# A graph network on one core: the last stage with its gate combined three groups ahead

## The chip, the core and the metric

The kernel runs on one core of a Trainium2 chip. A core has TensorE (matmuls and transposes into PSUM), VectorE, ScalarE and GpSimd (elementwise work), and SyncE, which here issues plain DMAs. GpSimd also issues the indirect DMAs (gathers and scatters by row numbers). Each engine runs its own list of instructions in order and waits on semaphores for the others. The metric is the device time of the whole kernel in microseconds. In the profile PE is TensorE, PEld its weight loads, DVE VectorE, ACT ScalarE, POOL GpSimd, SP SyncE.

## What is computed

Two layers of a heterogeneous graph transformer over 6250 nodes of width 128 and 100000 edges, with 16 node types and 32 edge types, and at the end a dense layer, a sum with the input and a layer norm. What matters here is what is done to each node once the sums over its edges are there:

```python
h = silu(typed_linear(hag, ntype, Wa))        # hag: attention-weighted messages, summed by node
alpha = sigmoid(skip[ntype])[:, None]
h = h * alpha + x * (1.0 - alpha)
mu, var = mean(h), mean((h - mu) ** 2)
h = (h - mu) * rsqrt(var + 1e-05) * g + b
...                                            # after the second layer:
out = layernorm(x_input + h @ ff_w + ff_b)
```

## The kernel before

The nodes are sorted by type and padded to 64 tiles of 128 nodes, so that a tile has one type and a typed linear map is one matmul with a weight picked by the type. A fused pass makes tables and queries of a layer, and an attention pass (`attend`) goes over the edges. After the second layer's attention comes the last stage, the functions named `finish` of each engine. It works on 16 groups of 4 tiles (`GROUP`, `GROUPS`). The change lies in this stage alone.

For a group g the stage does, engine by engine, in the names of the code:

- SyncE `load(g)`: three loads (edge sums, h of the layer before, x) into a ring of 8 places. From group 8 on it waits for the sum with x of group g - 8.
- VectorE `divide_in(g)` (L1666 to L1668): divides the sums by their totals.
- TensorE `turn_in(g)` (L1274): four transposes; ScalarE `turn_in(g)` (L1007) copies them out of PSUM bank 0; TensorE `project_in(g)` (L1282): the typed linear map.
- ScalarE `scale_o_res(g)` (L1022): h of before times 1 - alpha, four instructions; ScalarE `gate(g)` (L1029): the tanh that the silu is made of.
- VectorE `combine(g)` (L1812, L1817, and `statistics` with L1673, L1677, L1679): gate, residual, mean and variance.
- GpSimd `power` (L807): one instruction raises variances to the power -1/2. It takes up to two of them at once: the layer's, of a group ahead, and the output's, of group g.
- VectorE `shift(g)` (L1825): minus mean times that power; ScalarE `centre(g)` (L999): the normalised rows, four instructions.
- TensorE `turn_hn(g)` (L1291): four transposes; ScalarE `turn_hn(g)` (L1013) copies them from bank 2 with g and b; TensorE `spread_bias(g)` (L1297), a matmul with one row that puts the bias into the output's bank, and `project_out(g)` (L1303), the dense layer.
- VectorE `add_x(g)` (L1833 and `statistics`): the sum with x and its mean and variance; the output's half of `power(g)`; VectorE `output_shift(g)` (L1842); ScalarE `normalise(g)` (L1036), four instructions; GpSimd `scatter(g)` (L813), four indirect DMAs.

The order is written out by hand: on each engine a loop over steps i calls these functions for groups at different distances from i. In step i VectorE adds x of group i and combines group i + 2; TensorE and ScalarE turn in group i + 3 and turn out group i + 1; power(i) takes the output's variance of group i and the layer's of group i + 2. `wait_ge(semaphore, n)` holds an engine until n increments are there; `wait(engine, semaphore, n)` does so where n is positive.

Of the kernel before, what the change touches and what calls it, by code (L numbers as in the profile page):

```python
# [24 lines left out]
GROUP = 4  # L25
GROUPS = SORTED_TILES // GROUP
# [35 lines left out]
EPS = 1e-5  # L62
# [28 lines left out]
def gnn_kernel(nc, x, src, dst, etype, ntype, Wk, Wq, Wv, Wa, Watt, Wmsg, pri, skip, ln_g, ln_b, ff_w, ff_b, out):  # L91
# [5 lines left out]
    with ctx:  # L97
# [604 lines left out]
        def _(pool):  # L702
# [92 lines left out]
            def finish():  # L795

                def power(g):

                    layer, output = g + 2 < GROUPS, g >= 0
                    if layer:  # L800
                        pool.wait_ge(var_ready, GROUPS + g + 3)
                        wait(pool, hn_ready, GROUPS + g + 1 if g >= 0 else 0)
# [14 lines left out]
                for i in range(-2, GROUPS + 2):  # L817
                    if 0 <= i - 2 < GROUPS:
                        scatter(i - 2)
                    if i < GROUPS:  # L820
                        power(i)
# [55 lines left out]
        def _(act):  # L877
# [112 lines left out]
            def finish():  # L990
# [3 lines left out]
                def centre(g):  # L994
# [3 lines left out]
                    for t in range(GROUP):  # L998
                        ins = nc.scalar.activation(o_hn[:, g % 2, t], o_h[:, g % 3, t], ACT.Identity,  # L999
                                                   scale=rstd[:, g % 2, 0, t:t + 1], bias=hn_shift[:, g % 2, t:t + 1])  # L1000
# [40 lines left out]
                for i in range(-3, GROUPS + 2):  # L1041
                    if real(i + 1):
                        centre(i + 1)
                    if real(i + 3):
                        turn_in(i + 3)
                    if real(i + 1):
                        turn_hn(i + 1)
                    if real(i + 3):
                        scale_o_res(i + 3)
                        gate(i + 3)  # L1050
                    if real(i - 1):
                        normalise(i - 1)

# [60 lines left out]
        def _(pe):  # L1114
# [149 lines left out]
            def finish():  # L1264
# [42 lines left out]
                for i in range(-3, GROUPS):  # L1307
                    if real(i + 3):
                        types = tile_types((i + 3) * GROUP, GROUP)
                        turn_in(i + 3)  # L1310
                    if real(i + 1):
                        turn_hn(i + 1)
                    if real(i + 3):
                        project_in(i + 3, types)
                    if real(i + 1):
                        spread_bias(i + 1)
                        project_out(i + 1)
# [103 lines left out]
        def _(dve):  # L1421
# [248 lines left out]
            def statistics(par, kind, tiles, mean_var_, ready):  # L1670
# [8 lines left out]
                v.tensor_scalar(var_eps[:, par, kind], mean_var_[:, par, :, 1], EPS, None, ALU.add).then_inc(ready, 1)  # L1679
# [118 lines left out]
            def finish():  # L1798
# [7 lines left out]
                def combine(g):  # L1806
# [12 lines left out]
                    statistics(g % 2, 0, lambda t: hh[:, t], mean_var, var_ready)  # L1819
# [248 lines left out]
```

## Time and profile before

| | |
|---|---|
| median of 3 runs | 3597.92 us (3592.7 to 3605.9) |
| the profiled execution | 3599.04 us, its span 3597.2 us |
| mean granted TensorE clock | 0.843 |
| busy in the span: VectorE, GpSimd, TensorE | 76%, 69%, 69% |
| last stage, first load to end of span | 3429.75 to 3597.2 us |
| issued in it: group 3's and group 15's turn_in copy | 3454.87 and 3550.68 us |

A row of a timeline gives start, duration, engine, line, operation and tiles, how many instructions of a kind in a row are put together, and in square brackets how long the engine was idle before it and what ended that. The granted clock (PEclk) is 1.00 at 2.4 GHz and 0.50 at 1.2 GHz. Busy times of matmuls can overlap a little, as their ends are modelled.

### The profile page before, as it was taken

What the parts mean: (1) busy time and instruction counts of PE and PEld (TensorE: products, weight loads), DVE (VectorE), ACT (ScalarE), POOL (GpSimd) and SP (SyncE); (2) the same over time, 40 slices, a digit from 0 to 9 for tenths busy, and PEclk for the clock granted to TensorE, in tenths of its full rate; (3) what the DMA queues carried; (4) which work ended last, traced back from release to release, by engine and by line L of the source; (5) the groups of instructions that cost most, each with busy time, mean ns of one, the idle gap of its engine ahead of it and who ended that gap; (6) DMA issues with size and microseconds to landing.
All of it is one profiled execution on the core that took longest, in us unless ns stands there. A gap on an engine that the chain in (4) does not pass through costs nothing.

```text
span 3597.2 us, 61645 instructions
## 1 busy us (share of the span) xinstructions
PE 2472.3 (69%) x14287; PEld 1814.4 (50%) x14288; DVE 2746.2 (76%) x6153; ACT 1893.1 (53%) x4824; POOL 2474.7 (69%) x2501
## 2 busy tenths in 40 slices
PE   2777777467767767667677777657777776767665
PEld 1333333356666656666333333346666665666543
DVE  7667677488888878787687888758888888888765
ACT  1667677145444544545576767615445445544555
POOL 3666665677777777774566666477777777777746
PEclk8889988688888888888799999868888888888866
DMA  7999999655555545445799999955554555555350
GB/s 152 404 391 395 373 391 401 214 151 146 150 151 152 147 140 144 137 140 147 196 407 382 383 371 374 400 177 138 143 142 140 143 143 141 143 140 142 92 154 33
DMA packets 331216, 783.28 MB, mean 218 GB/s; under 512 B 87275, under 2 KB 262267, under 8 KB 318335
## 3 DMA queue, kind: packets, MB, share of 16 engines
q0 software_dynamic: 106016, 638.52, 49.5%
q1 hardware_dynamic: 216371, 139.98, 14.8%
q8 instruction: 139, 2.28, 0.3%
q14 instruction: 242, 1.98, 0.2%
q10 hardware_dynamic: 8448, 0.53, 0.2%
HBM read 335.84 MB, written 573.22 MB: 253 GB/s over the span
## 4 chain that ended last, share of the span: by engine, by line
POOL 26%; DMA 20%; issue 20%; DVE 11%; PE 10%; ACT 5%; DVEq 5%; POOLq 3%; ACTq 0%; SPq 0%
POOL region L836 21%; DMA relation_table<-region,scatter_node 13%; DMA region<-relation_table,key_of 5%; PE bank L1178 4%; ACT region L924 3%; DVEq L1893 3%; POOLq L831 2%; PE bank L1345 2%; DVEq L1901 1%; DMA region_q<-sums_by_node,gather_node 1%; DVE region_q L1873 1%; POOL aggregated_rows L848 1%; PE bank L1208 1%; POOL region_q L741 1%; DVE region L1887 1%
## 5 line engine op out<-in xcount | busy, mean ns | idle before, releaser
L836 POOL DMA_INDIRECT region<-relation_table,key_of x1568 | 1567.7, 1000 | 501.0 <-issue 442.2
L1345 PE MATMUL bank<-region,arena 128*128 128x136 f32 x3968 | 717.9, 335 | 255.4 <-ACT arena L1063 146.6
L1345 PEld LDWEIGHTS bank<-region,arena 128*128 128x128 f32 x3968 | 620.9, 231 | 333.9 <-issue 221.6
L924 ACT COPY region<-bank 128x512 f32<-128x512 f32 x1152 | 621.9, 599 | 285.8 <-DMA relation_table<-region,scatter_node 167.2
L1690 DVE COPY region<-bank 128x512 f32<-128x512 f32 x896 | 585.9, 685 | 209.2 <-DMA relation_table<-region,scatter_node 121.1
L1178 PE MATMUL bank<-sums,arena 128*128 128x512 bf16 x2048 | 620.5, 414 | 172.8 <-ACT region L924 142.8
L1060 ACT ACTIVATE arena<-iota_free,minus_dst 128x128 f32<-128x128 f32 x1984 | 629.0, 387 | 168.1 <-PE bank L1345 166.1
L1334 PE MATMUL bank<-region_q 128*128 x3968 | 640.6, 315 | 78.0 <-DVE region_q L1873 54.0
L1334 PEld LDWEIGHTS bank<-region_q 128*128 128x128 f32 x3968 | 604.3, 232 | 85.5 <-issue 85.4
L1864 DVE TENSOR_TENSOR bank<-bank,region 128x512 f32<-128x512 f32 x496 | 346.0, 698 | 363.9 <-POOLq L844 193.2
L1068 ACT ACTIVATE region<-arena 128x32 f32<-128x32 f32 x496 | 106.6, 215 | 949.7 <-DVE arena L1977 938.7
L1178 PEld LDWEIGHTS bank<-sums,arena 128*128 128x128 bf16 x2048 | 194.1, 102 | 498.9 <-ACT region L924 222.6
L1887 DVE TENSOR_TENSOR region<-region 128x512 f32<-128x512 f32 x496 | 338.0, 681 | 19.8 <-issue 11.1
L1878 DVE TENSOR_REDUCE arena<-bank 128x32 f32<-128x512 f32 x496 | 335.7, 677 | 0.0
L1063 ACT ACTIVATE arena<-arena 128x512 f32<-128x512 f32 x496 | 312.4, 630 | 15.7
L1873 DVE TENSOR_SCALAR region_q<-arena,row_no 128x512 f32<-128x512 bf16 x496 | 245.9, 497 | 39.8 <-issue 19.8
L757 POOL TENSOR_TENSOR sums<-arena,sums 128x256 f32<-128x256 f32 x128 | 86.2, 673 | 230.1 <-ACT arena L942 229.6
L1378 PE MATMUL bank<-ident,arena 128*1 128x128 f32 x496 | 124.8, 409 | 104.0 <-DVE arena L1942 104.0
L1697 DVE COPY arena<-bank 128x1024 bf16<-128x1024 bf16 x256 | 175.5, 685 | 22.3 <-PE bank L1199 15.5
L1199 PEld LDWEIGHTS bank<-identb,sums 128*128 128x128 bf16 x2048 | 151.8, 106 | 56.1 <-issue 17.6
L1199 PE MATMUL bank<-identb,sums 128*128 128x128 bf16 x2048 | 174.8, 234 | 2.6 <-POOL sums L761 2.6
L774 POOL DMA_INDIRECT relation_table<-region,scatter_node x128 | 126.2, 986 | 70.2 <-issue 35.1
(299 smaller groups left out, 2801.9 us busy)
## 6 DMA issues: line engine op xcount, KB each, us to landing
arena<-edge_places SPq DMA_DIRECT2D x496, 128.0 KB, 3.2
region<-relation_table,key_of POOLq DMA_INDIRECT x1568, 3.0
arena<-segment_flags SPq DMA_DIRECT2D x124, 128.0 KB
region_q<-q_rows SPq DMA_DIRECT2D x6, 768.0 KB, 15.7
aggregated_rows<-one_less_alpha SPq DMA_DIRECT2D x17, 256.0 KB, 4.0
region<-aggregated_rows SPq DMA_DIRECT2D x16, 272.0 KB, 3.1
sums<-relation_weight_parts SPq DMA_DIRECT2D x32, 128.0 KB, 9.9
x_sorted<-arena SPq DMA_DIRECT2D x16, 256.0 KB, 13.6
```

Source lines behind the costliest of these rows:

```text
L836: pool.indirect_dma_start(out=rows[:, r, s], out_offset=None, in_=table, in_offset=bass.IndirectOffsetOnAxis(ap=key_of[:, n:n + 1], axis=0 ...
L924: nc.scalar.copy(stage[:, r, :, k * HS:(k + 1) * HS], bank[TABLE_BANK + k % TABLE_BANKS][:, :].rearrange("p (t o) -> p t o", t=RT)).then_i ...
L1060: chain.step(nc.scalar.activation(onehots[:, at, s], iota_free[:, :], ACT.Abs, bias=minus_dst[:, bass.ds(block_.b * BLOCK + (q * QUAD + s) ...
L1063: nc.scalar.activation(onehots[:, at], onehots[:, at], ACT.Relu, scale=-1.0, bias=1.0).then_inc(onehot_ready, 1)
L1178: nc.tensor.matmul(bank[TABLE_BANK + k % TABLE_BANKS][:, :], x_spreadT[:, k, :], w_rel[:, k, :], start=True, stop=True).then_inc(table_psu ...
L1199: ins = nc.tensor.transpose(bank[SPREAD_BANK[half]][:, :].bitcast(BF16)[:, k * P:(k + 1) * P], x_spread[:, tile.par, half * H + k].rearran ...
L1334: ins = nc.tensor.matmul(bank[Q_BANK[at]][:, s * D:(s + 1) * D], onehotT[:, at, s], q_rows[:, bass.ds(tile, 1), :].rearrange("p a n -> p ( ...
L1345: ins = nc.tensor.matmul(bank[SUM_BANK[q % SUM_RING]][:, 0:SUMC], onehots[:, at, s], weighed_rows[:, weighed_at, s, :], start=(s == 0), st ...
L1690: v.tensor_copy(stage[:, r, :, k * HS:(k + 1) * HS], bank[TABLE_BANK + k % TABLE_BANKS][:, :].rearrange("p (t o) -> p t o", t=RT)).then_in ...
L1864: v.tensor_tensor(fetched, fetched, rows[:, bass.ds(read, 1), :, 0:D].rearrange("p r s d -> p (r s) d"), ALU.mult).then_inc(prod_ready, 1)
L1878: v.tensor_reduce(score[:, block_.par, q * QUAD:(q + 1) * QUAD, :], bank[Q_BANK[q_place(block_, q)]][:, :].rearrange("p (s h o) -> p s h o ...
L1887: v.tensor_tensor(part[:, :, H:SUMC].rearrange("p s (h o) -> p s h o", h=H), msg, bc(part[:, :, 0:H], 3, HS), ALU.mult).then_inc(weighted, 1)
```

## The change

Three things, all in the last stage. Combine, and with it the layer's half of the power, is done three groups ahead of the output instead of two (and `divide_in` five ahead instead of four, TensorE's and ScalarE's turning in four ahead instead of three, their turning out two ahead instead of one). On VectorE the two shifts stand behind the sum with x instead of in front of it. And the order within a step of TensorE and ScalarE is another. Since a power now holds an output of group g and a layer of group g + 3, the layer's place in `var_eps` and `rstd` has the other parity.

```diff
@@ GpSimd, finish @@
-                    layer, output = g + 2 < GROUPS, g >= 0
+                    layer, output = g + 3 < GROUPS, g >= 0
                     if layer:
-                        pool.wait_ge(var_ready, GROUPS + g + 3)
-                        wait(pool, hn_ready, GROUPS + g + 1 if g >= 0 else 0)
+                        pool.wait_ge(var_ready, GROUPS + g + 4)
+                        wait(pool, hn_ready, GROUPS + g + 2 if g >= -1 else 0)
...
-                for i in range(-2, GROUPS + 2):
+                for i in range(-3, GROUPS + 2):
@@ ScalarE, finish @@
-                                                   scale=rstd[:, g % 2, 0, t:t + 1], bias=hn_shift[:, g % 2, t:t + 1])
+                                                   scale=rstd[:, (g + 1) % 2, 0, t:t + 1], bias=hn_shift[:, g % 2, t:t + 1])
...
-                for i in range(-3, GROUPS + 2):
-                    if real(i + 1):
-                        centre(i + 1)
-                    if real(i + 3):
-                        turn_in(i + 3)
-                    if real(i + 1):
-                        turn_hn(i + 1)
-                    if real(i + 3):
-                        scale_o_res(i + 3)
-                        gate(i + 3)
+                for i in range(-4, GROUPS + 1):
+                    if real(i + 4):
+                        turn_in(i + 4)
+                        scale_o_res(i + 4)
+                    if real(i + 2):
+                        centre(i + 2)
+                    if real(i + 4):
+                        gate(i + 4)
                     if real(i - 1):
                         normalise(i - 1)
+                    if real(i + 2):
+                        turn_hn(i + 2)
@@ TensorE, finish @@
-                for i in range(-3, GROUPS):
-                    if real(i + 3):
-                        types = tile_types((i + 3) * GROUP, GROUP)
-                        turn_in(i + 3)
-                    if real(i + 1):
-                        turn_hn(i + 1)
-                    if real(i + 3):
-                        project_in(i + 3, types)
-                    if real(i + 1):
-                        spread_bias(i + 1)
-                        project_out(i + 1)
+                for i in range(-4, GROUPS):
+                    if real(i + 4):
+                        types = tile_types((i + 4) * GROUP, GROUP)
+                        turn_in(i + 4)
+                        project_in(i + 4, types)
+                    if real(i + 2):
+                        turn_hn(i + 2)
+                        spread_bias(i + 2)
+                        project_out(i + 2)
@@ VectorE, finish @@
-                    dve.wait_ge(rstd_ready, GROUPS + g + 3)
+                    dve.wait_ge(rstd_ready, GROUPS + g + 4)
...
-                for i in range(-4, GROUPS + 1):
-                    if real(i + 1):
-                        shift(i + 1)
-                    if real(i - 1):
-                        output_shift(i - 1)
+                for i in range(-5, GROUPS + 1):
                     if real(i):
                         add_x(i)
                     if real(i + 2):
-                        combine(i + 2)
-                    if real(i + 4):
-                        divide_in(i + 4)
+                        shift(i + 2)
+                    if real(i - 1):
+                        output_shift(i - 1)
+                    if real(i + 3):
+                        combine(i + 3)
+                    if real(i + 5):
+                        divide_in(i + 5)
```

What stands in a row on ScalarE in one step of the middle of the stage, before (L1007 is turn_in, L1013 turn_hn, L1022 scale_o_res, L1029 gate, L1036 normalise, L999 centre; in brackets the semaphores waited for):

```order
L999 ACTIVATE region<-region,rstd 128x128 [waits hnT_psum,hn_shifted]
L999 ACTIVATE region<-region,rstd 128x128 x3
L1007 COPY region<-bank 128x512 [waits z_psum,inT_psum]
L1013 ACTIVATE region<-bank,affine 128x512 [waits out_psum,hnT_psum]
L1022 ACTIVATE region<-region,one_less_alpha 128x128 [waits layer_const_ready,rows_loaded3]
L1022 ACTIVATE region<-region,one_less_alpha 128x128 x3
L1029 ACTIVATE region<-bank 128x512 [waits z_used,z_psum]
L1036 ACTIVATE region<-region,out_shift,rstd 128x128 [waits scattered1,norm_ready]
L1036 ACTIVATE region<-region,out_shift,rstd 128x128 x3
```

And after, on ScalarE, from the end of one step over the next:

```order
L1013 ACTIVATE region<-bank,affine 128x512 [waits out_psum,hnT_psum]
L1007 COPY region<-bank 128x512 [waits z_psum,inT_psum]
L1022 ACTIVATE region<-region,one_less_alpha 128x128 [waits layer_const_ready,rows_loaded4]
L1022 ACTIVATE region<-region,one_less_alpha 128x128 x3
L999 ACTIVATE region<-region,rstd 128x128 [waits hnT_psum,hn_shifted]
L999 ACTIVATE region<-region,rstd 128x128 x3
L1029 ACTIVATE region<-bank 128x512 [waits z_used,z_psum]
L1036 ACTIVATE region<-region,out_shift,rstd 128x128 [waits scattered1,norm_ready]
L1036 ACTIVATE region<-region,out_shift,rstd 128x128 x3
L1013 ACTIVATE region<-bank,affine 128x512 [waits out_psum,hnT_psum]
L1007 COPY region<-bank 128x512 [waits z_psum,inT_psum]
```

The copy of turn_hn (L1013) has moved from the third place to the last of its step, directly in front of the next step's turn_in (L1007).

On TensorE, before, from the spread of one step on (L1274 is turn_in, L1291 turn_hn, L1282 project_in, L1297 spread_bias, L1303 project_out):

```order
L1297 MATMUL bank<-row_const,ones 128x512 [waits y_ready]
L1303 MATMUL bank<-region_q,region 128x128 [waits hnT_ready]
L1303 MATMUL bank<-region_q,region 128x128 x3
L1159 TENSOR_LOAD tile_type
L1274 MATMUL bank<-ident,region 128x128 [waits inT_ready,in_ready]
L1274 MATMUL bank<-ident,region 128x128 x3
L1291 MATMUL bank<-ident,region 128x128 [waits hnT_ready,hn_ready]
L1291 MATMUL bank<-ident,region 128x128 x3
L1282 ISA [waits z_used,inT_ready]
L1282 MATMUL bank<-region_q,region 128x128
```

And after, on TensorE, the same place:

```order
L1291 MATMUL bank<-ident,region 128x128 [waits hnT_ready,hn_ready]
L1291 MATMUL bank<-ident,region 128x128 x3
L1297 MATMUL bank<-row_const,ones 128x512 [waits y_ready]
L1303 MATMUL bank<-region_q,region 128x128 [waits hnT_ready]
L1303 MATMUL bank<-region_q,region 128x128 x3
L1159 TENSOR_LOAD tile_type
L1274 MATMUL bank<-ident,region 128x128 [waits inT_ready,in_ready]
L1274 MATMUL bank<-ident,region 128x128 x3
L1282 ISA [waits z_used,inT_ready]
L1282 MATMUL bank<-region_q,region 128x128
```

The transposes of turn_hn no longer stand between those of turn_in and project_in, but behind project_in.

## Rows read from the trace of the kernel before

**Rows 1.** Windows of the fill and the steady part: window, length, busy, clock, DMA.
```profile
core 0: us, PE busy (x) PEld busy (x) DVE busy (x) ACT busy (x) POOL busy (x), PEclk, DMA share, GB/s
3429.00:3456.00 27.00, 16.07 (x60) 12.54 (x61) 13.13 (x50) 11.64 (x29) 2.05 (x2) 0.50 0.82 241
3456.00:3551.00 95.00, 69.11 (x309) 49.04 (x309) 79.32 (x349) 71.11 (x176) 61.73 (x54) 0.77 0.31 91
```

**Rows 2.** Timeline of VectorE over one period: start, us, instructions, idle before.
```profile
3533.48 0.16 DVE L1825 SCALAR_TENSOR_TENSOR region<-mean_var,rstd 128x4 f32<-128x4 f32 x1 [0.59 <-POOL rstd L807]
...
3539.92 0.69 DVE L1668 TENSOR_TENSOR region<-region 128x512 f32<-128x512 f32 x1
3541.20 0.16 DVE L1825 SCALAR_TENSOR_TENSOR region<-mean_var,rstd 128x4 f32<-128x4 f32 x1 [0.59 <-POOL rstd L807]
```

**Rows 3.** Timeline of ScalarE over one period at the full clock.
```profile
3536.07 0.78 ACT L1013 ACTIVATE region<-bank,affine 128x512 f32<-128x512 f32 x1 [0.28 <-PE bank L1291]
3536.75 1.26 ACT L1022 ACTIVATE region<-region,one_less_alpha 128x128 f32<-128x128 f32 x4
3537.92 0.57 ACT L1029 ACTIVATE region<-bank 128x512 f32<-128x512 f32 x1
3538.40 1.64 ACT L1036 ACTIVATE region<-region,out_shift,rstd 128x128 f32<-128x128 f32 x4
3541.40 1.65 ACT L999 ACTIVATE region<-region,rstd 128x128 f32<-128x128 f32 x4 [1.37 <-DVE region L1825]
3542.95 0.56 ACT L1007 COPY region<-bank 128x512 f32<-128x512 f32 x1
```

**Rows 4.** Timeline of TensorE over one period at the full clock.
```profile
3535.38 0.65 PE L1291 MATMUL bank<-ident,region 128*128 128x128 f32 x4 [1.78 <-ACT region L999]
3535.95 1.15 PE L1282 MATMUL bank<-region_q,region 128*128 x8
...
3540.66 0.66 PE L1274 MATMUL bank<-ident,region 128*128 128x128 f32 x4 [1.43 <-DVE region L1668]
```

**Rows 5.** Timeline of TensorE and ScalarE at the half clock, two places.
```profile
3451.91 2.08 PE L1303 MATMUL bank<-region_q,region 128*128 128x128 f32 x8
...
3453.78 1.06 PE L1274 MATMUL bank<-ident,region 128*128 128x128 f32 x4
...
3454.87 0.59 ACT L1007 COPY region<-bank 128x512 f32<-128x512 f32 x1 [2.60 <-PE bank L1274]
...
3557.20 1.65 ACT L999 ACTIVATE region<-region,rstd 128x128 f32<-128x128 f32 x4 [1.26 <-DVE region L1825]
...
3558.90 1.12 PE L1291 MATMUL bank<-ident,region 128*128 128x128 f32 x4 [1.25 <-ACT region L999]
...
3559.95 2.07 PE L1297 MATMUL bank<-row_const,ones 1*128 1x512 f32 x2
...
3561.94 2.08 PE L1303 MATMUL bank<-region_q,region 128*128 128x128 f32 x8
```

**Rows 6.** Timeline: transposes of group 2, and group 15's turn_in copy.
```profile
3445.34 1.12 PE L1274 MATMUL bank<-ident,region 128*128 128x128 f32 x4 [1.73 <-DVE region L1668]
...
3550.68 0.56 ACT L1007 COPY region<-bank 128x512 f32<-128x512 f32 x1
```

**Rows 7.** Timeline of GpSimd in the tail.
```profile
3563.51 1.67 POOL L807 TENSOR_TENSOR rstd<-var_eps,minus_half 128x8 f32<-128x8 f32 x1 [1.40 <-DVE var_eps L1679]
3565.38 1.04 POOL L813 DMA_INDIRECT out_dram<-region,scatter_node  x1 [0.20 <-issue]
...
3576.45 1.07 POOL L807 TENSOR_TENSOR rstd<-var_eps,minus_half 128x4 f32<-128x4 f32 x1
3577.71 1.04 POOL L813 DMA_INDIRECT out_dram<-region,scatter_node  x1 [0.19 <-issue]
...
3586.72 0.97 POOL L813 DMA_INDIRECT out_dram<-region,scatter_node  x1 [0.30 <-issue]
```

**Rows 8.** Windows of two stretches at the half clock, columns as in rows 1.
```profile
3511.00:3520.00 9.00, 8.59 (x31) 6.45 (x32) 6.94 (x32) 6.98 (x17) 6.68 (x6) 0.50 0.40 121
...
3545.00:3575.00 30.00, 21.92 (x64) 13.74 (x64) 18.72 (x89) 18.40 (x45) 21.88 (x20) 0.50 0.07 26
```

More of the change, by code:

```diff
@@ L1668, in divide, with statistics @@
                 v.tensor_tensor(messages, messages, bc(total, 3, HS), ALU.mult).then_inc(in_ready, 1)
-            def statistics(par, kind, tiles, mean_var_, ready):
+            def statistics(par, kind, at, tiles, mean_var_, ready):
                 for t in range(GROUP):
@@ L1678, in statistics @@
                 chain.wait()
-                v.tensor_scalar(var_eps[:, par, kind], mean_var_[:, par, :, 1], EPS, None, ALU.add).then_inc(ready, 1)
+                v.tensor_scalar(var_eps[:, at, kind], mean_var_[:, par, :, 1], EPS, None, ALU.add).then_inc(ready, 1)
             def fused(l):
@@ L1818, in combine @@
                     chain.wait()
-                    statistics(g % 2, 0, lambda t: hh[:, t], mean_var, var_ready)
+                    statistics(g % 2, 0, (g + 1) % 2, lambda t: hh[:, t], mean_var, var_ready)
                 def shift(g):
@@ L1824, in shift @@
                     wait(dve, hn_ready, GROUPS + g - 1 if g >= 2 else 0)
-                    v.scalar_tensor_tensor(hn_shift[:, g % 2], mean_var[:, g % 2, :, 0], -1.0, rstd[:, g % 2, 0],
+                    v.scalar_tensor_tensor(hn_shift[:, g % 2], mean_var[:, g % 2, :, 0], -1.0, rstd[:, (g + 1) % 2, 0],
                                            ALU.mult, ALU.mult).then_inc(hn_shifted, 1)
@@ L1835, in add_x @@
                     dve.wait_ge(y_ready, g + 1)
-                    statistics(g % 2, 1, lambda t: y[:, t], out_mean_var, out_var_ready)
+                    statistics(g % 2, 1, g % 2, lambda t: y[:, t], out_mean_var, out_var_ready)
                 def output_shift(g):
-                    dve.wait_ge(rstd_ready, GROUPS + g + 3)
+                    dve.wait_ge(rstd_ready, GROUPS + g + 4)
                     wait(dve, out_ready, g - 1)
```

## The prediction

> **What bounds the kernel now.** I read the windows by stage first. The change touches only the last stage, from the loads at 3429.75 us to the end at 3597.2 us; the 3430 us before it run the same instructions. It has a fill at the half clock up to 3456, a steady part of 95 us and a tail. In the steady part VectorE is busy 79.3 us, ScalarE 71.1, TensorE 69.1, GpSimd 61.7 [rows 1], so several engines are nearly full and none is.
>
> Next I read the timeline of VectorE in one period. L1825 starts at 3533.48 after 0.59 us of idle time that ends with GpSimd's power, and again at 3541.20 after 0.59 [rows 2]. The period is 7.72 us, of which VectorE works from 3533.48 to the end of L1668 at 3540.61, that is 7.13. So in this stretch the path goes round VectorE and GpSimd: combine's variance, power (1.67 us, the first row of [rows 7]), shift, sum with x, combine. This is the wait the change removes. The copies of turn_in on ScalarE start at 3454.87 for group 3 [rows 5] and at 3550.68 for group 15 [rows 6]: 95.81 us for 12 periods, 7.98 on average. The excess over 7.72 comes with TensorE's lower clock. The granted clock averages 0.77 in the steady part [rows 1], and as it has only the levels 1.0 and 0.5 there (2.4 and 1.2 GHz), it was full in 0.27/0.50 = 54% of that time: some 6.7 periods of 7.72, so that the other 5.3 took 8.3 each.
>
> **What the change removes.** Combine of group g+3 now stands before power(g), and after combine VectorE has divide_in and the sum with x (over 3 us of the 7.13) before it needs the power. 1.67 us are covered, so the 0.59 us go. What would be late next on VectorE alone is its own work: 7.13 us plus some 0.02 of handover, 7.15 a period. The sum of VectorE's instructions is unchanged, and so is GpSimd's (one power more in the fill, and of the last output powers three instead of two have no layer part).
>
> **What it adds: a ring between ScalarE and TensorE.** ScalarE's row of a period is now turn_in, scale, centre, gate, normalise, turn_hn. TensorE's is turn_in, project_in, turn_hn, spread, project_out. Before, ScalarE's turn_hn copy stood third, with scale, gate and normalise behind it to cover project_out. Now it is the last of the step. TensorE's project_out waits for it; the next turn_in transposes are queued behind project_out; ScalarE's next turn_in copy waits for these transposes, and everything else of ScalarE is queued behind that copy. Nothing on either engine overlaps this stretch, whatever VectorE does, so one turn of the ring is a floor for the period.
>
> One turn at the full clock, start to start, from [rows 3, 4]. The ScalarE instructions overlap the next by 0.09 (gate is 0.57 long, 0.48 to the next): turn_in 0.56 - 0.09 = 0.47; scale 1.17 (3536.75 to 3537.92); centre 1.55 (3541.40 to 3542.95); gate 0.48; normalise, four instructions like centre's, 1.55; turn_hn to its end 0.78. That is 6.00. Handover to TensorE 0.05 (as from centre's end, 3557.20 + 1.65 = 3558.85, to L1291 at 3558.90, [rows 5]). project_out has the eight passes of L1282, busy 1.15, of which some 0.07 overlap the next instruction: 1.08. Transposes until the copy starts: 0.69 (L1291 at 3535.38, L1013 at 3536.07). Sum 6.00 + 0.05 + 1.08 + 0.69 = 7.82 us. This is 0.1 above the 7.72 of before: the wait for GpSimd is gone and a slightly longer one stands in its place.
>
> At the half clock a second way round is longer [rows 5]: turn_in 0.47, scale 1.17, centre until TensorE's transposes start 1.70 (3557.20 to 3558.90), transposes 1.05, spread 1.99 (3559.95 to 3561.94), project_out 1.87 (3451.91 to 3453.78), transposes until the copy 1.09 (3453.78 to 3454.87). Sum 9.34 us. By the first way it would be 6.00 + 0.05 + 1.87 + 1.09 = 9.01, so 9.34 decides; at the full clock the second way, with its four TensorE pieces halved, is the shorter one. Before, a period with this clock in it cost 8.3, because turn_in's and turn_hn's copies were both covered by TensorE's other work.
>
> **What is moved past queues.** On GpSimd a power stands between two groups of scatters as before. SyncE's load of group 8 waits for the sum with x of group 0, and divide_in of group 8 is now three steps behind that sum instead of four: three periods, over 20 us, still cover it. ScalarE's centre waits for VectorE's shift, which now stands behind the sum with x; in the ring VectorE has 7.82 - 7.15 = 0.7 us to spare a period and gets ahead of ScalarE, so I cost it at nothing; if that cover went, VectorE's own 7.15 us a period would bound, which is the third rival.
>
> **How often the clock is full.** That is the unknown of the sum. In the kernel before it rose behind stretches in which TensorE had hardly a gap, such as 3511 to 3520 with 8.59 us busy of 9.00 [rows 8], where turn_in, turn_hn, project_in and project_out of neighbouring steps run into one another. It fell where one short group of transposes stands between two idle times, 1.4 and 1.8 us in every full-clock period [rows 4]. In the tail, with 21.9 us busy of 30, it never rose [rows 8]. After the change, at the half clock, TensorE works 1.05 + 1.9 + 1.05 + 1.99 + 1.87 = 7.9 us of 9.34, and the rest is cut into two gaps, one for turn_in's copy before project_in and one for centre before turn_hn: no stretch of the step is as dense as 3511 to 3520, in any period. At the full clock these pieces halve and three gaps lie between them. I expect it to be mostly at 1.2 GHz. The ends are 12 periods at half (9.34) and the share of before, 1/(0.54/7.82 + 0.46/9.34) = 8.45. I take 9 periods at half and 3 at full, 107.5 us for 12, nearer to the upper end.
>
> The Trainium skill, "TensorE: Matmul & The Clock Gate" (HAM oscillation), says that the clock falls when TensorE has long idle gaps and stays up when work is issued without them. By that alone the change should help, for its gaps are shorter. Here it fell with gaps of 1.4 and 1.8 us and stayed low in a tail that was 73% busy, so the trace does not bear the rule out, and it stands behind the second rival below.
>
> **Fill.** Transposes of group 2 start at 3445.34 [rows 6], as before; the copy can start at 3445.34 + 1.09 = 3446.4 (no centre in front of it now). One turn at half clock brings group 3's copy to 3455.8, against 3454.87 before: 0.9 later.
>
> **Tail.** From group 15's copy on. Before: copy at 3550.68, last scatter issued by 3586.72 + 0.97 = 3587.69, 37.0 us, then 9.5 us to the end of the span, which stays. After: turn_in of group 15 is in step 11 and not 12, so six groups are still to be scattered from there. Normalise of group 10 is done 0.47 + 1.17 + 1.55 + 0.48 + 1.64 = 5.3 us behind the copy. Then GpSimd is the bound [rows 7]: four scatters take 4 x 1.287 = 5.15 (3577.71 to 3586.72 is seven spacings); six groups 30.9; power 12 with two parts 1.87 (3563.51 to 3565.38); powers 13 to 15 with one part 1.26 each (3576.45 to 3577.71), 3.8. Sum 5.3 + 30.9 + 1.9 + 3.8 - 0.3 (the last spacing) = 41.6 us.
>
> **Sum.** 3455.8 + 107.5 + 41.6 + 9.5 = 3614.4 us span, 17.2 over 3597.2. The profiled execution took 3599.04, so 3616.2 by its own time; over the median of 3597.92 it is 3615.1. I forecast 3616, slower by 0.5%. What a measurement of this kernel can tell from no change is about 0.5%, 18 us: the bound is 3615.9 and my forecast sits on it.
>
> **Rivals.** All with the same fill and tail, 3506.9 + 12 periods, and 0.7 added to the median.
> - The clock keeps its share of before: 12 x 8.45 = 101.4, span 3608.3, time 3609. For it: TensorE's work per period is the same. Against: the broken dense stretch.
> - The clock stays full once up, as shorter gaps could bring about: 12 x 7.82 = 93.8, span 3600.7, time 3601.5. For it: the longest gap is shorter. Against: it fell in [rows 1] with gaps of the same size. The rule cited above gives this case.
> - The ring does not bind and the work of VectorE does: 12 x 7.15 = 85.8, span 3592.7, time 3593.5, not slower, 0.1% faster. It needs the next turn_in transposes to be done without waiting for project_out, and decides if one turn is under 7.15. Against: [rows 5] show L1274 starting only behind L1303, and the waits are in the program's order.
> - The ring binds and the clock never rises, with a few tenths a period of jitter on top: 12 x 9.34 = 112.1 gives 3619.0, with 0.4 more each 3623.8; time 3620 to 3625.
>
> **How the numbers follow.** Forecast, 0 to 4 periods at full clock around the 9 at half: 0.60, own range 3611 to 3621, a bit more than half of it above 3615.9. Clock share as before 0.19; full clock 0.08; ring open 0.04; clock never up with more on top 0.09. Slower by over 0.5%: 0.36 + 0.09 + 0.03 of the second case = 0.48. Faster by over 0.5% would need periods of 6.3 us, less than VectorE's own work: 0.02 for what I have not seen. Within: 0.50. The range goes from 3602 (nearly all at full clock) to 3623 and leaves out the open ring and the extremes.
>
> **What would show it.** Right: VectorE's L1825 (L1823 then) no longer waits for GpSimd's rstd; ScalarE's turn_in copy waits for TensorE's transposes some 1.8 us at the full and 3 us at the half clock in every period, the largest wait of ScalarE; the transposes follow project_out with no gap; turn_in copies of groups 3 and 15 stand 94 to 112 us apart; the granted clock of the steady part is below 0.77; the tail from the last copy is 41 to 42 us, with GpSimd's scatters back to back. Wrong: a period under 7.8, a granted clock at or above 0.77, or VectorE being the engine that never waits.

## The result

| | before | after |
|---|---|---|
| median of 5 runs | 3599.92 us (3592.7 to 3605.9) | 3616.89 us (3609.74 to 3626.3) |
| span of the profiled execution | 3597.2 us | 3607.9 us |
| first load of the last stage | 3429.75 us | 3423.72 us |
| last stage, to the end of the span | 167.5 us | 184.2 us |
| group 3's to group 15's turn_in copy | 95.81 us | 107.05 us |

The ratio is 1.0046, with a 95% interval of 1.0029 to 1.0062: slower by 17 us. The two profiled executions differ by 10.7 us only, because the part in front of the last stage, which is the same in both, happened to be 6.0 us shorter in the second; the stage itself took 16.7 us more. So I compare stages, and never the spans. The 16.7 are 1.0 in the fill (first load to group 3's copy: 25.1 before, 26.1 after), 11.2 in the twelve periods, and 4.5 in the tail (from group 15's copy to the end of the last scatter's issue: 37.0 before, 41.5 after). The profiled execution is the shortest of the changed kernel's five.

ScalarE's timeline over two turns, of the changed kernel. It answers to [rows 3]; L1007 is turn_in, L1022 scale, L999 centre, L1029 gate, L1036 normalise, L1013 turn_hn:

```profile
3477.89 0.58 ACT L1007 COPY region<-bank 128x512 f32<-128x512 f32 x1 [3.38 <-PE bank L1274]
3478.38 1.28 ACT L1022 ACTIVATE region<-region,one_less_alpha 128x128 f32<-128x128 f32 x4
3479.55 1.64 ACT L999 ACTIVATE region<-region,rstd 128x128 f32<-128x128 f32 x4
3481.09 0.58 ACT L1029 ACTIVATE region<-bank 128x512 f32<-128x512 f32 x1
3481.57 1.64 ACT L1036 ACTIVATE region<-region,out_shift,rstd 128x128 f32<-128x128 f32 x4
3483.11 0.77 ACT L1013 ACTIVATE region<-bank,affine 128x512 f32<-128x512 f32 x1
3485.65 0.58 ACT L1007 COPY region<-bank 128x512 f32<-128x512 f32 x1 [1.77 <-PE bank L1274]
...
3495.01 0.58 ACT L1007 COPY region<-bank 128x512 f32<-128x512 f32 x1 [3.38 <-PE bank L1274]
```

In these turns ScalarE waits once, in front of turn_in, for TensorE's transposes: 1.77 us when the clock was full, 3.38 when it was half. (In the first two of the twelve periods, which have no normalise yet, that wait is 4.08, and the copy of turn_hn waits 0.7 too.) From 3477.89 to 3485.65 is one turn with the clock almost always full (mean 0.94), 7.76 us; from 3485.65 to 3495.01 one at the half, 9.36. Over the twelve periods ScalarE waited in front of turn_in, VectorE for the power in front of its shift, and GpSimd for normalise in front of the scatters (each row gives us in total, times, the longest):

```profile
ACT region L1007 <- PE bank L1274: 40.8, 13, 4.1
```
```profile
DVE region L1823 <- POOL rstd L807: 15.6, 9, 2.1
POOL out_dram L813 <- ACT region L1036: 21.6, 9, 2.8
```

The windows say of the twelve periods that the clock was 0.61 (0.77 in the steady part of [rows 1]):

```profile
3449.81:3556.86 107.05, 85.10 (x312) 57.94 (x312) 77.79 (x344) 68.91 (x173) 55.07 (x49) 0.61 0.27 78
```

TensorE's timeline of the same stretch (L1274 is turn_in, L1282 project_in, L1291 turn_hn, L1297 spread_bias, L1303 project_out) answers to [rows 4, 5]:

```profile
3471.88 1.11 PE L1291 MATMUL bank<-ident,region 128*128 128x128 f32 x4 [0.55 <-ACT region L999]
3472.93 2.07 PE L1297 MATMUL bank<-row_const,ones 1*128 1x512 f32 x2
3474.93 2.08 PE L1303 MATMUL bank<-region_q,region 128*128 128x128 f32 x8
3476.80 1.06 PE L1274 MATMUL bank<-ident,region 128*128 128x128 f32 x4
3478.63 1.15 PE L1282 MATMUL bank<-region_q,region 128*128 x8 [0.77 <-ACT region L1007]
3481.25 0.66 PE L1291 MATMUL bank<-ident,region 128*128 128x128 f32 x4 [1.47 <-ACT region L999]
3481.84 1.12 PE L1297 MATMUL bank<-row_const,ones 1*128 1x512 f32 x2
3483.93 1.16 PE L1303 MATMUL bank<-region_q,region 128*128 128x128 f32 x8 [0.97 <-ACT region L1013]
3484.92 0.69 PE L1274 MATMUL bank<-ident,region 128*128 128x128 f32 x4
```

Both ways round of the prediction can be seen: the first from the copy of turn_hn over project_out and turn_in's transposes, the second from centre over all four of TensorE's pieces. At the half clock (first four rows) TensorE runs from the transposes of turn_hn to turn_in's without a gap, so project_out does not wait for the copy of turn_hn: the second way decides. At the full clock project_out waits 0.97 us for L1013: the first way decides. turn_in's transposes follow project_out with no gap at either. Of the twelve periods only three have this wait, and they are the three short ones (7.76, 7.78 and 7.67 us):

```profile
PE bank L1303 <- ACT region L1013: 2.5, 3, 1.0
```

The chain of waits says the same in order of time: ScalarE's scale and centre, four pieces of TensorE, and round again.

```profile
3469.01 1.28 ACT region L1022 x4
3470.29 1.55 ACT region L999 x4
3471.84 0.04 issue
3471.88 1.11 PE bank L1291 x4
3473.00 2.00 PE bank L1297 x2
3475.00 2.01 PE bank L1303 x8
3477.00 0.87 PE bank L1274 x4
```

GpSimd's end answers to [rows 7]. From the copy at 3556.86 it is 41.5 us to 3597.38 + 0.97 = 3598.35:

```profile
3574.91 1.05 POOL L807 TENSOR_TENSOR rstd<-var_eps,minus_half 128x4 f32<-128x4 f32 x1
3576.15 1.04 POOL L813 DMA_INDIRECT out_dram<-region,scatter_node  x1 [0.19 <-issue]
...
3597.38 0.97 POOL L813 DMA_INDIRECT out_dram<-region,scatter_node  x1 [0.30 <-issue]
```

### The profile page after: what moved, and what is told of

It is laid out like the page before. It is cut to its first block, busy times and chain, and to the rows that moved or that the text cites. A ratio compares the mean times of both kernels' runs of the same rounds, so it can differ in the third digit from the quotient of the medians.

```text
span 3607.9 us, 61555 instructions
## 1 busy us (share of the span) xinstructions
PE 2475.4 (69%) x14196; PEld 1823.1 (51%) x14288; DVE 2750.1 (76%) x6153; ACT 1890.9 (52%) x4824; POOL 2474.1 (69%) x2502
## 4 chain that ended last, share of the span: by engine, by line
POOL 25%; DMA 21%; issue 20%; PE 11%; DVE 9%; ACT 6%; DVEq 5%; POOLq 3%; SPq 0%; ACTq 0%
POOL region L836 21%; DMA relation_table<-region,scatter_node 13%; DMA region<-relation_table,key_of 5%; PE bank L1178 4%; ACT region L924 3%; DVEq L1891 3%; POOLq L831 2%; DMA region_q<-sums_by_node,gather_node 2%; PE bank L1343 1%; DVEq L1899 1%; POOL aggregated_rows L848 1%; DVE region_q L1871 1%; POOL region_q L741 1%; PE bank L1208 1%; DVE region L1885 1%
## 5 line engine op out<-in xcount | busy, mean ns | idle before, releaser
L1178 PE MATMUL bank<-sums,arena 128*128 128x512 bf16 x1957 | 596.0, 414 | 184.4 <-ACT region L924 134.4
L1862 DVE TENSOR_TENSOR bank<-bank,region 128x512 f32<-128x512 f32 x496 | 345.8, 697 | 361.6 <-POOLq L844 174.3
L1871 DVE TENSOR_SCALAR region_q<-arena,row_no 128x512 f32<-128x512 bf16 x496 | 247.7, 500 | 39.5 <-issue 19.6
```

What stands on the lines that cost most here:

```text
L1178: nc.tensor.matmul(bank[TABLE_BANK + k % TABLE_BANKS][:, :], x_spreadT[:, k, :], w_rel[:, k, :], start=True, stop=True).then_inc(table_psu ...
L1862: v.tensor_tensor(fetched, fetched, rows[:, bass.ds(read, 1), :, 0:D].rearrange("p r s d -> p (r s) d"), ALU.mult).then_inc(prod_ready, 1)
```

## The experiments

Each run is given with the time between the turn_in copies of groups 3 and 15 (twelve periods) in its profiled execution, read from windows cut at these two copies, and with its ratio to the kernel before, run beside it. Columns of a row of windows as in [rows 1].

Two cautions. The first of the twelve periods lies in a stretch in which ScalarE has no normalise yet, and in some versions it is much shorter than the rest, so the table gives the mean of the other eleven too. And the last stage began between 3423.7 and 3442.3 us in the profiled executions, though all that comes before it is the same; so lengths of the stage are compared.

| version | ratio | last stage, us | first period | mean of the other eleven | tail |
|---|---|---|---|---|---|
| kernel before | 1 | 167.5 | 8.39 | 7.95 | 37.0 |
| changed kernel | 1.0046 | 184.2 | 9.36 | 8.88 | 41.5 |
| three ahead, old step order | 0.9977 | 161.3 | 4.89 | 7.29 | 41.0 |
| ring alone | 1.0041 | 180.1 | 7.24 | 9.18 | 38.4 |
| changed, filler | 1.0000 | 167.9 | 6.79 | 7.86 | 41.5 |
| turn_hn in front of normalise | 1.0066 | 190.6 | 9.36 | 9.36 | 42.8 |
| no bias | 1.0039 | 181.9 | 8.06 | 8.88 | 41.4 |
| centre in front of scale | 1.0028 | 174.3 | 7.47 | 8.43 | 41.4 |
| both ways opened | 1.0005 | 170.4 | 6.12 | 7.88 | 42.4 |
| three ahead, old order, shifts in front | 0.9992 | 164.6 | 4.53 | 7.74 | 42.4 |
| shifts behind, two ahead | 1.0078 | 200.5 | 9.26 | 10.28 | 39.5 |
| three ahead, old order, filler | 0.9976 | 163.1 | 7.11 | 7.50 | 41.4 |

### Three groups ahead, step order of before

```diff
# changed kernel, ScalarE (and TensorE: turn_in, turn_hn, project_in, spread_bias, project_out)
-                    if real(i + 4):
-                        turn_in(i + 4)
-                        scale_o_res(i + 4)
                     if real(i + 2):
                         centre(i + 2)
                     if real(i + 4):
+                        turn_in(i + 4)
+                    if real(i + 2):
+                        turn_hn(i + 2)
+                    if real(i + 4):
+                        scale_o_res(i + 4)
                         gate(i + 4)
                     if real(i - 1):
                         normalise(i - 1)
-                    if real(i + 2):
-                        turn_hn(i + 2)
```

> Three groups ahead and the shifts behind the sum with x, as in the change; ScalarE's and TensorE's order within a step as before (centre, turn_in, turn_hn, scale, gate, normalise; turn_in, turn_hn, project_in, spread, project_out). Theory (the ring between ScalarE and TensorE made the change slow, not the depth): the ring is gone, VectorE's own work bounds at 7.15 us at the full clock and TensorE's at about 7.9 at the half clock, 7.1 to 7.6 us between turn_in copies on average, the tail 41 to 42 us from the last copy; 5 to 10 us less than the kernel before, ratio 0.997 to 0.999. Rival (the depth itself costs, by one more group in flight, a longer fill and a longer tail): as slow as the changed kernel, 15 to 19 us over the kernel before, ratio 1.004 to 1.005.

Measured: ratio 0.9977 (0.9968 to 0.9986), median 3593.93 us against 3603.23 of the kernel before on the same chip.

```profile
3456.48:3541.55 85.07, 60.95 (x312) 43.84 (x310) 76.50 (x336) 70.12 (x172) 56.96 (x49) 0.87 0.34 98
```

VectorE's wait for the power, in the kernel before and in this version:

```profile
DVE region L1825 <- POOL rstd L807: 7.0, 12, 0.6
```
```profile
DVE region L1825 <- POOL rstd L807: 1.9, 5, 0.6
```

The twelve periods take 7.09 us on average, but the first is 4.89 and the other eleven average 7.29, against 7.95 before; of the six with the clock at 0.99 or 1.00, three are 7.05 to 7.11 and three 7.48 to 7.71. The tail is 41.0 us, so 4.0 of the 10.7 us that the twelve periods gain are given back there. The depth and the place of the shifts together take away most of the wait: this version beats both kernels, by 9 and by some 25 us. The rival is out. What makes the change slow is the order within the step.

### The ring alone

```diff
# kernel before, ScalarE (and TensorE: turn_in, project_in, turn_hn, spread_bias, project_out)
-                    if real(i + 1):
-                        centre(i + 1)
                     if real(i + 3):
                         turn_in(i + 3)
-                    if real(i + 1):
-                        turn_hn(i + 1)
-                    if real(i + 3):
                         scale_o_res(i + 3)
+                    if real(i + 1):
+                        centre(i + 1)
+                    if real(i + 3):
                         gate(i + 3)
                     if real(i - 1):
                         normalise(i - 1)
+                    if real(i + 1):
+                        turn_hn(i + 1)
```

> The kernel before, two groups ahead and the shifts in front, but ScalarE's order within a step turn_in, scale, centre, gate, normalise, turn_hn and TensorE's turn_in, project_in, turn_hn, spread, project_out. Theory (the ring alone): 9.35 us between turn_in copies at the half clock and about 7.8 at the full one, mean granted clock of the steady part under 0.65, 12 to 18 us over the kernel before, ratio 1.0035 to 1.005. Rival (depth): same as the kernel before, ratio 0.999 to 1.001.

Measured: ratio 1.0041 (1.0028 to 1.0054).

```profile
3461.45:3569.66 108.21, 86.44 (x312) 58.56 (x312) 80.23 (x350) 70.36 (x176) 61.56 (x54) 0.61 0.27 80
```

Nine of the twelve periods are 9.36 or 9.37 us, one with the clock nearly always full (0.95) is 7.66. With two groups ahead and the old place of the shifts, the step order by itself costs what the whole change costs. The tail is 38.4 us here.

### The clock held up by idle work

```diff
# changed kernel, TensorE; filler(n): n transposes of the identity into PSUM bank 5
                         turn_in(i + 4)
+                        filler(2)
                         project_in(i + 4, types)
                     if real(i + 2):
+                        filler(4)
                         turn_hn(i + 2)
                         spread_bias(i + 2)
+                        filler(2)
                         project_out(i + 2)
```

> The changed kernel, with eight idle transposes a step on TensorE into a PSUM bank that nobody reads: two in front of project_in, four in front of turn_hn, two in front of project_out. They lie in TensorE's gaps at the full clock. Theory (half of the loss is the clock: the ring takes 9.35 us at 1.2 GHz and 7.8 at 2.4): the clock stays up in most of the steady part, mean granted clock over 0.9, 7.8 to 8.2 us between turn_in copies, 8 to 14 us less than the changed kernel, ratio to the kernel before 1.000 to 1.003. Rival (the clock is only a symptom, TensorE's pieces are waited for by others anyway): more work on TensorE, and the time is that of the changed kernel or more, ratio 1.0045 or above.

Measured: ratio 1.0000 (0.9992 to 1.0009).

```profile
3460.84:3554.04 93.20, 69.44 (x410) 49.79 (x408) 77.83 (x342) 68.92 (x172) 57.02 (x50) 0.95 0.31 90
```

TensorE does work that nobody needs, which shortens its three gaps in a full-clock turn from 0.77, 1.47 and 0.97 us to 0.55, 1.03 and 0.61, and the kernel is 17 us faster than the changed one. Seven periods are 7.66 or 7.67 us, two at the start 6.8, and three in which the clock dipped 8.6 to 8.7. The two of 6.8 have no normalise: there the first way is 1.55 us shorter. So the ring with its clock up costs as much per period as the kernel before at the full clock (7.72); with the clock held at 0.95 none of the loss of 11.2 us in the twelve periods is left.

### The copy of turn_hn in front of normalise

```diff
# changed kernel, ScalarE
+                    if real(i + 2):
+                        turn_hn(i + 2)
                     if real(i - 1):
                         normalise(i - 1)
-                    if real(i + 2):
-                        turn_hn(i + 2)
```

> The changed kernel with ScalarE's turn_hn copy in front of normalise instead of behind it. This opens the first way round (copy of turn_hn, project_out, turn_in) and leaves the second (scale, centre, transposes, spread, project_out, turn_in). Theory (two ways round, the second decides at the half clock): 9.35 us between turn_in copies at the half clock as in the changed kernel, and at the full clock under 7.3, so the time depends on the clock: 3 to 19 us over the kernel before, ratio 1.001 to 1.005. Rival (only the place of the turn_hn copy counts): 7.2 to 8 us at both clocks, at or under the time of the kernel before.

Measured: ratio 1.0066 (1.0052 to 1.0080), above the upper end that I gave.

```profile
3451.10:3563.37 112.27, 93.73 (x312) 63.73 (x312) 78.33 (x344) 69.98 (x172) 55.35 (x49) 0.54 0.26 75
```

All twelve periods are 9.30 to 9.37 us: opening the first way gains nothing while the second decides, as forecast. In three of them the clock was 0.67 or 0.68 on average and not 0.50, and they are no shorter: it was full during project_in only, which is not on the second way. A period near 7.3 at the full clock, the other half of the forecast, did not occur, so no run shows it. I had not thought that this version could be slower than the changed kernel. In its profiled execution it had no period near 7.8 (the changed kernel had three), and its tail is 42.8 us, 1.3 longer, with normalise behind the copy; 5.2 + 1.3 = 6.5 us are about the 0.0020 by which the ratios differ. Why its clock rose less I did not settle.

### The spread of the bias left out

```diff
# changed kernel, TensorE; the output lacks the dense layer's bias
-                    nc.tensor.matmul(bank[OUT_BANK[g % 2]][:, :], ones[0:1, :], bias_row, start=True, stop=False)
...
-                                               o_hnT[:, g % 2, t], w_ff, start=False, stop=(t == GROUP - 1))
+                                               o_hnT[:, g % 2, t], w_ff, start=True, stop=True)
```

> The changed kernel without TensorE's spread of the bias (the dense layer's bias is left out of the output), 1.99 us of TensorE a step at the half clock. Theory (two ways round): the second way loses these 1.99 us and the first, 6.00 + 0.05 + 1.87 + 1.09 = 9.0 us, decides, so a period at the half clock falls from 9.36 to 9.0 only, and one at the full clock stays at 7.8; 3 to 12 us less than the changed kernel, depending on how often the clock is full. Rival (TensorE's work at the half clock adds up in a row): a period at the half clock falls by the full 2 us to 7.4.

Measured: ratio 1.0039 (1.0025 to 1.0054), not told apart from the changed kernel's 1.0046 (the 3 us are at the low end of what was expected).

```profile
3460.09:3565.81 105.72, 68.42 (x288) 56.13 (x288) 80.35 (x347) 68.93 (x173) 56.36 (x51) 0.56 0.27 80
```

Nine of the twelve periods are 9.06 or 9.07 us. Two microseconds of TensorE's work are gone and the period falls by 0.30: the other way round, worked out as 9.0, takes over. The time gains little, as behind the first two only one period was short here (7.73), where the changed kernel had three.

### Centre in front of scale, and both ways opened

```diff
# changed kernel, ScalarE; the second version has turn_hn in front of normalise too
                         turn_in(i + 4)
-                        scale_o_res(i + 4)
                     if real(i + 2):
                         centre(i + 2)
                     if real(i + 4):
+                        scale_o_res(i + 4)
                         gate(i + 4)
```

> The changed kernel with ScalarE's centre in front of scale. The second way round loses scale's 1.17 us (8.2 at the half clock), the first has the same pieces as before, 9.0. Theory: a period at the half clock is 9.0 and one at the full clock 7.8, four to nine us less than the changed kernel, ratio 1.002 to 1.004. Rival (only the place of the turn_hn copy matters, or the sum of ScalarE's work): no difference from the changed kernel, ratio 1.0045.

> The changed kernel with centre in front of scale and the turn_hn copy in front of normalise: both ways round are shorter than at least one other. At the half clock TensorE's own row with the wait for turn_in's copy is left: 1.09 + 0.56 + 0.2 + 1.87 + 1.05 + 1.99 + 1.87 = 8.6 us; at the full clock VectorE's 7.15. Theory: periods of 8.6 and 7.15, time by the clock between 8 us under and 4 us over the kernel before, ratio 0.998 to 1.001, and under both one-sided versions. Rival (normalise behind turn_hn delays the scatters, which bound): as e4_turn_hn_first, ratio 1.005 or more.

Measured: centre first, ratio 1.0028 (1.0018 to 1.0039); both, 1.0005 (0.9991 to 1.0018). The windows of the one and of the other:

```profile
3455.42:3555.61 100.19, 76.48 (x312) 54.15 (x312) 80.28 (x354) 68.69 (x173) 58.25 (x51) 0.69 0.29 84
```
```profile
3457.97:3550.74 92.77, 77.43 (x312) 55.05 (x312) 77.65 (x342) 68.99 (x173) 56.41 (x49) 0.67 0.30 90
```

With centre first six periods are 9.00 us, the first way; the others have the clock full for part or most of the time. With both opened the last six, all at the half clock, are 8.55 or 8.56, and the row of TensorE shows what is left: its own work with one wait for turn_in's copy.

```profile
3541.09 1.06 PE L1274 MATMUL bank<-ident,region 128*128 128x128 f32 x4
3542.92 2.07 PE L1282 MATMUL bank<-region_q,region 128*128 x8 [0.77 <-ACT region L1007]
3544.78 1.06 PE L1291 MATMUL bank<-ident,region 128*128 128x128 f32 x4
3545.77 2.07 PE L1297 MATMUL bank<-row_const,ones 1*128 1x512 f32 x2
3547.77 2.08 PE L1303 MATMUL bank<-region_q,region 128*128 128x128 f32 x8
```

So the half-clock period went 9.36, 9.00, 8.55 as one way after another was opened, each time to the next sum. The forecast of 7.15 for the full clock was not met: the first five periods alternate between 6.12 us (clock 0.98) and 7.47 (0.79), 6.66 on average and less than the 7.15 of VectorE. I take it that early in the stage the turning-in can run ahead of VectorE for a few groups; no run tests that.

### The place of the shifts, with and without the third group

```diff
# first experiment (three ahead, old step order), VectorE: shifts in front again
+                    if real(i + 2):
+                        shift(i + 2)
+                    if real(i - 1):
+                        output_shift(i - 1)
                     if real(i):
                         add_x(i)
-                    if real(i + 2):
-                        shift(i + 2)
-                    if real(i - 1):
-                        output_shift(i - 1)
```
```diff
# kernel before (two ahead), VectorE: shifts behind
-                    if real(i + 1):
-                        shift(i + 1)
-                    if real(i - 1):
-                        output_shift(i - 1)
                     if real(i):
                         add_x(i)
+                    if real(i + 1):
+                        shift(i + 1)
+                    if real(i - 1):
+                        output_shift(i - 1)
```

> Three groups ahead with the step order of the kernel before on ScalarE and TensorE (as in e1_old_step_order), and the two shifts in front of the sum with x as in the kernel before. Theory (the depth alone doesn't cover the power; its place behind the sum with x does): VectorE has only divide_in between combine and the shift, as before, so it waits some 0.5 us a period and the period is 7.3 to 7.7; 2 to 6 us under the kernel before, ratio 0.9985 to 0.9995, and 3 to 7 us over e1_old_step_order. Rival (the depth is what helps): as e1_old_step_order, ratio 0.9977.

> The kernel before with one edit: the two shifts behind the sum with x, two groups ahead and all else as it was. Theory: the sum with x of group i+1 then waits for a chain that begins with the shift of the same group one step earlier: shift 0.15, centre 1.70, transposes, project_in, spread, project_out (3.9 us at the full clock, 7.0 at the half), and the sum's own 2.24 stand in front of the next shift: 8.1 us a period at the full clock and 11.1 at the half, so 5 to 35 us over the kernel before, ratio 1.002 to 1.009. That is why the change needs its third group. Rival (the place of the shifts covers the power by itself): 7.2 us a period, under the kernel before.

Measured: three ahead with the shifts in front, ratio 0.9992 (0.9981 to 1.0003), 12 periods in 89.62 us against 85.07 with the shifts behind. VectorE waits for the power as in the kernel before (6.5 us in all, 11 times), and behind a first period of 4.53 us the other eleven average 7.74. Shifts behind with two groups, ratio 1.0078 (1.0064 to 1.0092), 12 periods in 122.39 us, those with more of the full clock (0.82 to 0.84) 9.1 to 9.5 and the others 10.7 to 11.2; its VectorE waits before the sum with x, 34.2 us in all, 11 times:

```profile
3505.33 0.69 DVE L1833 TENSOR_TENSOR region<-bank,region 128x512 f32<-128x512 f32 x1 [3.57 <-PE bank L1303]
```

Each of the two edits alone brings nothing or does harm: the third group with the shifts in front is not told apart from the kernel before (at most 0.2% faster), the shifts behind with two groups cost 0.8%. Only together do they give the 0.23% of the first experiment.

### The good version with filler

```diff
# first experiment, TensorE
+                        filler(3)
                         turn_in(i + 4)
                     if real(i + 2):
+                        filler(4)
                         turn_hn(i + 2)
```

> e1_old_step_order (three groups ahead, step order of before) with seven idle transposes a step on TensorE, three in front of turn_in and four in front of turn_hn, into a PSUM bank that nobody reads. Theory (the clock costs only where TensorE is on a way that bounds): the granted clock rises from 0.87 towards 1.0, but VectorE bounds at 7.1 us, so the period goes from 7.09 to between 7.0 and 7.15 and the time is that of e1_old_step_order, ratio 0.997 to 0.999. Rival (the clock was still costing some 0.3 us a period in e1): 3 us or more under e1_old_step_order, ratio 0.9965 or below.

Measured: ratio 0.9976 (0.9966 to 0.9985), as without filler; the rival's 3 us are not there. But the reason that I gave is not borne out in its profiled execution: the clock was 0.85 and not higher, and the twelve periods took 89.59 us, three of them 7.7 to 8.5 with the clock at 0.50 to 0.59, where the filler lengthens TensorE's row.

```profile
3464.85:3554.44 89.59, 71.48 (x398) 54.97 (x397) 79.57 (x351) 69.98 (x174) 57.14 (x50) 0.85 0.32 94
```

Filler of the same kind raised the clock in one step order and, in this one profile, not in the other. That profile is of the longest of the eleven executions (3607.27 us, the median is 3594.32), mostly because its last stage began 11.5 us later than the first experiment's; the stage is 163.1 us against 161.3, with a shorter fill and longer periods. It shows that the time is the same, not why.

## Why the prediction was right

Forecast 3616 us, measured 3616.89; the change of 17.2 us in the sum, 16.7 in the stage of the two profiles. The mechanism was right. That the figure came out within 1 us is partly luck: the five executions of the changed kernel spread over 17 us, and two terms of the sum vary from run to run, the number of short periods and the fill.

- **The ring.** Forecast as the floor of a period, 7.82 us at the full and 9.34 at the half clock; measured 7.67 to 7.78 and 9.36. At the full clock the sum was a little long, as project_out took 0.99 us (3483.93 to 3484.92) and not 1.08, and the floor holds only for steps with a normalise: with filler two periods without one were 6.8. The one-edit experiments show it as the cause: without it the change is 25 us faster, and alone it costs 15 us. That two ways go round, and which decides at which clock, is shown by the waits of project_out (none at the half clock, up to 0.97 us in the three short periods) and by three experiments that stopped at 9.06, 9.00 and 8.55 us where 9.0, 9.0 and 8.6 were worked out.
- **The clock.** Forecast 9 periods at half and 3 at full, 107.5 us; measured 107.05: eight of 9.3 to 9.4, three of 7.7 to 7.8 and one of 9.0. That it was three is the lucky part: the ring alone had two at the full clock (7.24 and 7.66), and the version with turn_hn in front of normalise none. The filler shows what the clock is worth: with it at 0.95, 93.2 us. My reason, that the dense stretch is broken, was only argued; no run took the density alone. The case in which the clock stays up, 3601.5 us, did not come. In the turn before it fell, at 3485, TensorE's gaps were 0.77, 1.47 and 0.97 us; with filler they were 0.55, 1.03 and 0.61, and it stayed up for most of the time. The Trainium skill ("TensorE: Matmul & The Clock Gate", HAM oscillation) ties the fall to long idle gaps; gaps of this size were enough here, so the trace does not bear that out.
- **Fill and tail.** Fill 26.05 us forecast (3455.8 less 3429.75), 26.09 measured; so close a hit is luck, as the fill was 23.6 to 26.1 us in the versions that keep the ring. Tail 41.6 and 41.5. Most of the tail's 4.5 us comes with the third group and not with the ring: the tail is 41.0 to 42.8 in all versions three groups ahead, and 37.0, 38.4 and 39.5 in those with two. It was in the sum, but I did not say that about a quarter of the loss is the price of the third group and not of the ring.
- **What was wrong.** I expected that L1823 would no longer wait for GpSimd's power. It waits up to 2.1 us a period, 15.6 in all, more than the 0.59 of [rows 2]. VectorE gets there early, and GpSimd's power now stands behind scatters that wait for ScalarE's normalise: 21.6 us in nine waits, where the scatters of the kernel before have no such wait between the same two copies. The power starts only when the last scatter's issue ends:

```profile
3478.78 0.97 POOL L813 DMA_INDIRECT out_dram<-region,scatter_node  x1 [0.30 <-issue]
3479.75 1.70 POOL L807 TENSOR_TENSOR rstd<-var_eps,minus_half 128x8 f32<-128x8 f32 x1
```

  It costs nothing while the ring bounds, and in the first experiment, where the ring is gone, it shrank to 1.9 us over the twelve periods. The cover that I reckoned with (divide_in and the sum with x) covers the power's duration, not a power that starts late. The 8.3 us that I gave for a half-clock period of the kernel before is an average of two kinds: the three periods wholly at the half clock took 7.86, 8.01 and 7.87 us, and the one behind each, with the clock at 0.90, took 8.44, 8.32 and 8.42. The sum does not use it.
- **The step that the change was about.** 0.59 us a period, 7.0 in all, were to go; with the old step order 1.9 are left. The third rival, VectorE's 7.15 as the bound, needs that order, and comes near: the best full-clock periods took 7.05 to 7.11, the average behind the first was 7.29.

## What to carry to other kernels

When engines hand work to each other in a fixed order, add up every closed way round: each engine's last instruction of a step, what it releases, and what that one queues in front of. A way that closes within one step is a floor that no lookahead moves (here 9.36 us with two groups ahead and with three). Put a copy that another engine waits for early in its step and fill the rest behind it; and reckon a way at both clocks, since another may be the longest at the lower one.

## What was not expected of the hardware

Useless work made a kernel faster: eight idle transposes a step raised the mean granted clock from 0.61 to 0.95 and took the twelve periods from 107.05 to 93.20 us. In the version with the old step order, seven of them left the time as it was, and the clock at 0.85 where it was 0.87, by one profile of each.
